# Value items' low parts behind the last counts, four pairs of one-hots instead of seven from ScalarE, one query low part later

## The reference

```python
h = relu(layernorm(x))
q, k, v = h @ Wq + bq, h @ Wk + bk, h @ Wv + bv
adj = zeros((N, N)).at[src, dst].set(1.0)
a = q @ k.T / sqrt(512)
a = a * adj + (1.0 - adj) * -1e6
x = x + softmax(a) @ v
h = relu(layernorm(x))
# deg = edges per dst, loops included; w = deg**-0.5 at both ends
h = agg(h @ W1 + b1)          # agg: segment sum over src of w * h[dst]
h = relu(gamma * (h - mean) / sqrt(var + eps) + beta)
x = x + agg(h @ W2 + b2)
```

## Time and profile before

| | |
|---|---|
| median of 3 runs | 307.28 us (307.28 to 307.28) |
| profiled execution | 307.32 us |
| its span, first to last instruction | 305.5 us |
| granted TensorE clock | 1.00 throughout |
| TensorE busy | 295.5 us, 97% |
| VectorE busy | 207.0 us, 68% |
| ScalarE busy | 159.9 us, 52% |
| GpSimd busy | 57.6 us, 19% |

### The profile page before, as it was taken

The page is one execution under the profiler, slowest core; times in us unless marked ns, Lnnn a source line. Parts: engine busy times, 40 slices in busy tenths (PEclk is TensorE's granted clock), DMA queues, the critical chain, the costliest instruction groups (busy, mean ns, idle before and its releaser), DMA issues.

```text
span 305.5 us, 4845 instructions
## 1 busy us (share of the span) xinstructions
PE 295.5 (97%) x1345; PEld 227.3 (74%) x1345; DVE 207.0 (68%) x458; ACT 159.9 (52%) x266; POOL 57.6 (19%) x103
## 2 busy tenths in 40 slices
PE   7999889899999999999999999999999999999995
PEld 6777356466665888888888888887888888878884
DVE  3899999999977557965748575568344388276311
ACT  3999967989546546445444544357523044342000
POOL 5361353000000530032131420203010044100000
PEclk9999999999999999999999999999999999999999
DMA  7806040000600309444362625313102000000321
GB/s 256 311 23 186 1 141 0 1 0 2 207 0 3 69 3 238 79 95 89 85 148 43 150 40 104 67 38 69 34 20 52 0 3 0 0 2 0 111 98 69
DMA packets 42312, 21.67 MB, mean 71 GB/s; under 512 B 35760, under 2 KB 36016, under 8 KB 42288
## 3 DMA queue, kind: packets, MB, share of 16 engines
q1 hardware_dynamic: 41744, 20.33, 26.0%
q10 hardware_dynamic: 544, 1.05, 0.9%
HBM read 10.88 MB, written 2.10 MB: 42 GB/s over the span
## 4 chain that ended last, share of the span: by engine, by line
PE 86%; DVE 7%; issue 2%; DMA 1%; DVEq 1%; ACT 1%; ACTq 0%
PE ps L989 20%; PE ps L991 19%; PE ps L990 19%; PE ps L1242 10%; PE ps L1165 8%; PE ps L1055 8%; DVE src_oh L705 2%; DMA qk_raw<-L_gnn_Wk_in 1%; PE ps L1023 1%; DVE dst_oh L707 1%; DVEq L705 1%; DVE WT L688 1%; DVE T L809 0%; DVE smx L813 0%; DVE p L821 0%
## 5 line engine op out<-in xcount | busy, mean ns | idle before, releaser
L705 DVE TENSOR_SCALAR src_oh<-iota,ecol 128x512 f16 x135 | 40.0, 349 | 3.0 <-PE ps L1055 2.5
L1055 PE MATMUL ps<-src_oh,dst_oh 128*128 x135 | 34.0, 382 | 3.7 <-DVE dst_oh L707 3.3
L1165 PE MATMUL ps<-cnt,qh 128*128 128x512 f32 x128 | 30.1, 391 | 0.3 <-ACT cnt L575 0.3
L1055 PEld LDWEIGHTS ps<-src_oh,dst_oh 128*128 x135 | 13.3, 103 | 21.9 <-issue 12.5
L1242 PE MATMUL ps<-qh,cnt 128*128 128x512 f32 x128 | 29.3, 390 | 0.0
L1165 PEld LDWEIGHTS ps<-cnt,qh 128*128 128x128 f32 x128 | 23.9, 188 | 5.6 <-DVE qh L868 0.7
L1242 PEld LDWEIGHTS ps<-qh,cnt 128*128 128x128 f32 x128 | 24.0, 188 | 5.3 <-DVE vb L970 0.3
L991 PE MATMUL ps<-v,pT 128*128 128x512 f32 x64 | 25.0, 390 | 0.0
L989 PE MATMUL ps<-v,pT 128*128 128x512 f32 x64 | 24.9, 389 | 0.0
L989 PE MATMUL ps<-hT,qh 128*128 128x512 f32 x64 | 24.9, 389 | 0.0
L990 PE MATMUL ps<-v,pT 128*128 128x512 f32 x64 | 24.9, 389 | 0.0
(11 more groups left out here) (186 smaller groups left out, 685.2 us busy)
## 6 DMA issues: line engine op xcount, KB each, us to landing
xt<-x_in SPq DMA_DIRECT2D x16, 256.0 KB, 3.3
out<-xt SPq DMA_DIRECT2D x8, 256.0 KB, 2.1
qk_raw<-L_gnn_Wk_in ACTq DMA_DIRECT2D x2, 512.0 KB, 5.0
qk_raw<-L_gnn_Wq_in SPq DMA_DIRECT2D x2, 512.0 KB, 6.8
wB_raw<-L_gnn_Wv_in SPq DMA_DIRECT2D x2, 512.0 KB, 9.0
wB_raw<-L_gnn_W_in SPq DMA_DIRECT2D x2, 512.0 KB, 4.1
w_raw<-L_gnn_W_in SPq DMA_DIRECT2D x2, 512.0 KB, 4.6
bias_row<-L_gnn_b_in SPq DMA_DIRECT2D x2, 256.0 KB, 4.7
```

What stands on the lines that cost most here:

```text
L705: dve.tensor_scalar(src_oh[:, bass.ds(slot, 1), j, :].rearrange("p a n -> p (a n)"), iota[:, :], ecol[:, bass.ds(c + j, 1)], None, ALU.is_ ...
L1055: m = pe.matmul(ps[:, i % 2, :], dst_oh[:, bass.ds(slot, 1), :, j].rearrange("p a n -> p (a n)"), lead_oh[:, i % 2, j, :] if first and ACT ...
L1165: m = pe.matmul(bank(g), qh[:, d, a, c * P:(c + 1) * P], cnt[:, d, n * HALF:(n + 1) * HALF], start=(d == 0 and a == 1), stop=last)
```

## The change

1. The low part of each of the eight value items leaves `lo_of`. ScalarE, in `hi_of`, makes a second copy of the item from PSUM, `v_raw`, in the place in SBUF where the low part is to stand, right behind the high part's copy. VectorE subtracts later, from SBUF to SBUF (`v_lo`): blocks 0 to 5 behind the low part of ("q", 1, 0), blocks 6 and 7 in turn 0 of the blocks, behind `large_flag`. TensorE's first weighted sum waits for all eight.
2. A bank that held a value item is free once `v_raw` is made; item_lo counts only the other items (`left_bank`, `nth_lo`).
3. GpSimd's additions of bv wait for six of the eight v_lo.
4. ScalarE makes the pairs of windows 3, 5, 7 and 9 alone; windows 4, 6 and 8 get their src one-hots from VectorE, and GpSimd picks the columns of four windows instead of seven.
5. VectorE makes the low part of ("q", 0, 3) (ahead[13]) behind the one-hots of window 15 instead of before them.

```diff
-ACT_LEADS = 3
-ACT_LAST = 10
+ACT_LEADS = (3, 5, 7, 9)
...
+    v, v_raw, zT, edge_i, edge_f, chunk1, hit, reach = shared(
+        [("v", [P, NT, 2, D], F32R)], [("v_raw", [P, NT, 2, D], F32)], [("zT", [P, 2, KC, N], F32R)],
...
+    def left_bank(b, end):
+        before = [other for other in items[:end] if item_bank(other) == b]
+        if not before:
+            return None
+        if before[-1][0] == "v":
+            return S["v_raw"], before[-1][1] + 1
+        return S["item_lo"], nth_lo(before[-1])
...
-        for i in range(ACT_LEADS, ACT_LAST):
+        for i in ACT_LEADS:
             lead_columns(i)
...
+        pool.wait_ge(S["v_lo"], 6)
         for t in range(XT):
             add_bv(t)
...
                 act.activation(item_dest(item, 0), item_ps(item), ACT.Copy).then_inc(S["item_hi"], 1)
+            if what == "v":
+                act.activation(v_raw[:, n, 1, :], item_ps(item), ACT.Copy).then_inc(S["v_raw"], 1)
...
-            if ACT_LEADS <= i + 1 < ACT_LAST:
+            if i + 1 in ACT_LEADS:
                 lead_onehots(i + 1)
...
             what, n, c = item
+            if what == "v":
+                return
...
+        def v_lo(blocks):
+            for n in blocks:
+                dve.wait_ge(S["item_hi"], nth(("v", n, 0)))
+                dve.wait_ge(S["v_raw"], n + 1)
+                dve.tensor_tensor(v[:, n, 1, :], v_raw[:, n, 1, :], v[:, n, 0, :].bitcast(F32),
+                                  ALU.subtract).then_inc(S["v_lo"], 1)
...
-            chunks_of(i, first, LEAD, not ACT_LEADS <= i < ACT_LAST)
+            chunks_of(i, first, LEAD, i not in ACT_LEADS)
...
         for i in range(2, NW):
-            for item in ahead[i - 2]:
+            for item in ahead[i - 2] if i < NW - 1 else []:
                 lo_of(item)
...
-        for i in range(NW - 2, NW):
+        for i in range(NW - 3, NW):
             for item in ahead[i]:
                 lo_of(item)
...
         lo_of(("q", 1, 0))
+        v_lo(range(0, 6))
...
                 large_flag()
+                v_lo(range(6, NT))
                 p16_lo(0)
...
-            if last_in(item_bank(item), i - 1):
-                pe.wait_ge(S["item_lo"], last_in(item_bank(item), i - 1))
+            left = left_bank(item_bank(item), i - 1)
+            if left:
+                pe.wait_ge(*left)
...
             pe.wait_ge(S["p_lo"], t + 1)
+            if t == 0:
+                pe.wait_ge(S["v_lo"], NT)
```

More of the change, by code:

```diff
@@ L164, in gnn_kernel @@
     Wk_in0 Wk_in1 Wq_in0 Wq_in1 wB_in0 wB_in1 w2_in0 w2_in1 w_hi w_lo
-    x_sums x_means x_squares ln_scale ln_coef h_ready item_ps item_hi item_lo uw_ready hw_second fill_ready
+    x_sums x_means x_squares ln_scale ln_coef h_ready item_ps item_hi item_lo v_raw v_lo uw_ready hw_second fill_ready
     ncol_ready lead_cols lead_dist lead_made onehots onehots_used c_done c16 loops_added adj_in0 adj_in1 adj_in2 adj_in3
@@ L187, in gnn_kernel @@
     nth = lambda item: items.index(item) + 1
+    split_items = [item for item in items if item[0] != "v"]
+    nth_lo = lambda item: split_items.index(item) + 1
     item_bank = lambda item: start.get(item, final.get(item, 2 + (items.index(item) - len(start)) % ITEM_BANKS))
-    last_in = lambda b, end: max([n for n, other in enumerate(items[:end], 1) if item_bank(other) == b] + [0])
+    def left_bank(b, end):
[5 more added lines that the diff above has]
+        return S["item_lo"], nth_lo(before[-1])
     drel = lambda i: (drel_first if i < NW // 2 else drel_second)[:, i % (NW // 2), :]
@@ L468, in lead_onehots @@
         def lead_onehots(i):
-            n = i - ACT_LEADS + 1
+            n = ACT_LEADS.index(i) + 1
             act.wait_ge(S["lead_cols"], n)
             for j in range(LEAD):
-                act.activation(lead_oh[:, i % 2, j, :], iota[:, :], ACT.Abs,
+                act.activation(lead_oh[:, n % 2, j, :], iota[:, :], ACT.Abs,
                                bias=lead_col[:, i, j:j + 1]).then_inc(S["lead_dist"], 1)
             act.wait_ge(S["lead_dist"], LEAD * n)
-            act.activation(lead_oh[:, i % 2, :, :], lead_oh[:, i % 2, :, :], ACT.Relu, bias=ones[:, 0:1],
+            act.activation(lead_oh[:, n % 2, :, :], lead_oh[:, n % 2, :, :], ACT.Relu, bias=ones[:, 0:1],
                            scale=-1.0).then_inc(S["lead_made"], LEAD)
@@ L744, in mask_level @@
                 dve.wait_ge(S["uw_ready"], 4)
-                dve.wait_ge(S["item_lo"], nth(("w", 0, 0)))
+                dve.wait_ge(S["item_lo"], nth_lo(("w", 0, 0)))
             else:
@@ L1026, in make @@
             if what == "m":
-                pe.wait_ge(S["item_lo"], nth(("t", Q, n)))
+                pe.wait_ge(S["item_lo"], nth_lo(("t", Q, n)))
             else:
-                pe.wait_ge(S["item_lo"], nth(("h", n if what == "v" else 4 * n + 3, 0)))
+                pe.wait_ge(S["item_lo"], nth_lo(("h", n if what == "v" else 4 * n + 3, 0)))
             if item == ("v", 0, 0):
@@ L1055, in chunks @@
                 m = pe.matmul(ps[:, i % 2, :], dst_oh[:, bass.ds(slot, 1), :, j].rearrange("p a n -> p (a n)"),
-                              lead_oh[:, i % 2, j, :] if first and ACT_LEADS <= i < ACT_LAST else
+                              lead_oh[:, (ACT_LEADS.index(i) + 1) % 2, j, :] if first and i in ACT_LEADS else
                               src_oh[:, bass.ds(slot, 1), j, :].rearrange("p a n -> p (a n)"), start=first and j == 0,
@@ L1065, in counts @@
                 pe.wait_ge(S["c16"], 2 * (i - 1))
-            if ACT_LEADS <= i < ACT_LAST:
-                pe.wait_ge(S["lead_made"], LEAD * (i - ACT_LEADS + 1))
+            if i in ACT_LEADS:
+                pe.wait_ge(S["lead_made"], LEAD * (ACT_LEADS.index(i) + 1))
             first, end = bounds & (NCH - 1), bounds >> 8
@@ L1107, in scores @@
                 pe.wait_ge(S["c16"], 2 * NW)
-                pe.wait_ge(S["item_lo"], nth(("q", 0, KC - 1)))
+                pe.wait_ge(S["item_lo"], nth_lo(("q", 0, KC - 1)))
             if t == 4:
-                pe.wait_ge(S["item_lo"], len(items))
+                pe.wait_ge(S["item_lo"], len(split_items))
             if t >= 2:
@@ L1173, in _ @@
                 pe.wait_ge(S["degm_ready"], 1)
-                pe.wait_ge(S["item_lo"], last_in(6, nth(("q", 1, 0))))
+                pe.wait_ge(*left_bank(6, nth(("q", 1, 0))))
                 pe.transpose(bank(6)[:, 0:P], degm[:, 0:1].to_broadcast([P, P]), ident[:, :]).then_inc(S["degm_ps"], 1)
```

2 lines of the change are left out of this document (removed).

## The result

| | before | after |
|---|---|---|
| median | 307.28 us (307.17 to 308.27, 5 runs) | 310.03 us (309.12 to 310.31, 5 runs) |
| ratio | 1 | 1.0066, 95% interval 1.0046 to 1.0085 |
| profiled execution | 307.32 us | 310.03 us |
| its span | 305.5 us | 308.1 us |

The sign was right, the size was not: +2.75 where +0.75 was forecast, outside the range of 306.9 to 309.1. (The ratio is not the quotient of the two medians, which is 1.0089.) Both kernels' times fall into two groups some 1.1 us apart, and in the traces these groups differ in start-up (before: 47 of its 82 runs in four sets are in the lower group; after: 4 of 11 in two sets); the after profile is of the upper group where the before profile is of the lower. Lower group against lower group, after is about 309.0 and before about 307.25: +1.75 is what the changed kernel takes more, start-up aside.

The account below looks back on a forecast made before the run. TensorE, busy 97% of the span, was taken as the bound, so only its holes counted. Terms +1.36 (values), -0.66 (query), +0.05 (GpSimd) and 0 gave +0.75 on 307.32: 308.07 profiled, 308.0 median; range 306.9 to 309.1.

Parts of the forecast that it names:

- mechanism of the windows: Windows 5, 7, 9: v_raw ahead of ScalarE's pair delays the pair 0.49 us, and TensorE's groups with it; taken 1.36.
- the query's low part: Window 15: moving the low part of (0,3) behind the one-hots gains 0.66 us, bounds 0.55 to 1.05.
- the low parts behind the counts: Behind the counts, VectorE's eight moved subtractions fit into two stalls and cost 0 while nothing stretches them.
- Values in windows 5, 7 and 9: The extra ScalarE copy delays these windows by 0.49, 0.45 and 0.42 us, 1.36 together, bounds 1.08 and 1.47.
- The 0.13 that I let the step between two copies absorb: Window 7: a copy's row is 0.13 us longer than its pitch; that may go, leaving 0.36 to 0.49 of delay.
- The reading of the sequencer: Window 5: after waiting for the pair, TensorE's sequencer issues one loop turn in 1.07 us; only work queued earlier hides it.
- One-hots back on VectorE: Windows 4, 6, 8: six one-hots, 1.8 us, cost nothing because VectorE is ahead after 5.4 us of subtractions removed.
- it takes 96.07 to 96.73 out of the chain: Window 15: without the low part, VectorE's last one-hots and then TensorE's last group come 0.66 us earlier.
- GpSimd: End of window 2: fewer column copies start the window targets earlier, slowing VectorE's one-hots by 0 to 0.2 us, taken 0.05.
- rival A: Behind the counts: GpSimd's additions block VectorE's last two low parts, TensorE loses 0.53 us, 308.6 in all; chance 0.25.
- Both fit: Behind the counts: six low parts (3.66 us) and two (1.22) fit VectorE's stalls of 4.06 and 1.78, by 0.40 and 0.56.
- What I held against A: A one-hot begun inside a GpSimd operation grew by only 0.09 us (0.50 against 0.41), not by the operation's rest.

Follow-up runs that it names:

- e4: The changed kernel with ScalarE's copy v_raw behind the pair of one-hots of the same turn instead of before it: 307.70 us, ratio 0.9996.
- e2: The kernel before with four pairs by ScalarE (windows 3, 5, 7, 9) instead of seven, all else as before: 307.48 us, ratio 1.0002.
- e3: The kernel before with only the low part of query item (0,3) moved behind window 15's one-hots: 307.47 us, ratio 0.9993.
- k5: e4 with window 5's pair of one-hots made by VectorE, ScalarE keeping windows 3, 7 and 9: 307.58 us, ratio 1.0001.
- e1: The change's value items' part alone, with ScalarE's seven pairs and the query item's low part as in the kernel before: 309.89 us, ratio 1.0072.
- k7: e4 without the wait of GpSimd's additions for the sixth low part, so they run beside VectorE's low parts: 313.71 us, ratio 1.0166.
- k9: e4 with GpSimd's four additions waiting for the second masking in place of the sixth low part: 308.59 us, ratio 1.0026.
- k11: The changed kernel with 8 one-column stores on VectorE behind the first mask: 309.48 us, ratio 1.0053.
- k6: The kernel before with window 5's pair made by VectorE and the query item's low part behind window 15's one-hots: 307.24 us, ratio 0.9981.
- k8: The kernel before with 16 one-column stores on VectorE behind the first mask: 308.49 us, ratio 1.0014.
- k10: k6 with 8 one-column stores on VectorE behind the first mask: 306.55 us, ratio 0.9970.

## Why the prediction was wrong, step by step

The mechanism of the windows was right. Two terms of the sum failed, the query's low part (0.22 for 0.66) and the low parts behind the counts (0.42 for 0), and two stages that the sum left out added 0.35 (the last) and 0.92 (start-up).

- **Values in windows 5, 7 and 9: right.** Forecast +0.49, +0.45, +0.42 with 1.47 as the upper bound; measured +0.49, +0.51, +0.48, 1.48. The 0.13 that I let the step between two copies absorb was not absorbed. The reading of the sequencer held: groups at 1.07, and the second group of window 7 is 0.51 late once the shift of 1.21 ahead of the window is taken out (68.63 to 70.35). e4 takes all of it away with the one copy.
- **One-hots back on VectorE: right**, 0 (e2: -0.12, all in window 3, which has none of the six).
- **The query's low part: mis-sized.** The step that failed is "it takes 96.07 to 96.73 out of the chain". It took VectorE's data path as the limit and forgot the lesson that I had drawn for TensorE from the earlier trace rows: an engine can stand idle on its sequencer, and work in front hides it. The low part had hidden 0.36 us of idle time, and the step between the one-hots went from 1.00 to 0.77. Of 0.66, 0.22 came (0.19 in e3's window 15), outside my 0.55 to 1.05. The 0.36 is no fixed price: in k5 it is 0.10, and 0.47 came. Why, is open; that it changes with instructions elsewhere is like the last stage's branch, but no run tested it here.
- **GpSimd: wrong sign, small, cause not shown.** Forecast +0.05, measured -0.17. With three copies of the lead columns fewer, the window targets begin at 42.19 where the earlier trace rows has 43.35, start-up's 0.92 included. But e1 has all seven copies, its targets begin at 43.23, and its windows 2 to 4 still gain 0.14; e2 gains 0.13 there. So the earlier targets needn't be the reason.
- **Low parts behind the counts: rival A happened.** Forecast 0; measured +0.42 at the first weighted sum, A's price was 0.53. The step that failed is "Both fit": the six did (4.06 us held them, and the masking was not late), the last two did not. The additions stretched the identity's addition by 0.58 and the two low parts by some 0.6, together more than the 0.72 that the prediction had to spare. A had expected one wait of 1.25 there; it came in two pieces. What I held against A, a one-hot that grew by only 0.09 beside GpSimd, was another case: a one-hot of 128x384 in f16 beside a GpSimd operation on 132 columns. Why that one hardly waits and a low part beside an addition of 512 fp32 columns does, no run shows. The Trainium skill, "SBUF — State Buffer", section "SBUF: two separate sides", says that a VectorE operation with two SBUF inputs (beside a GpSimd one that reads SBUF) or in a two-port mode and a GpSimd one exclude each other for a whole instruction. For the low parts the trace agrees (1.70 us per pair of operations in k7), for the one-hot of the earlier trace rows it doesn't (0.50 for 0.41), and for p_lo with its one input (1.80 for 0.69 in k9) no row shows the mode. Had I taken A as the case, the forecast would have been 308.6, still 1.4 under the result.
- **The last stage: not in the sum at all.** +0.35 from a stage whose code the change does not touch (k11 takes it out with eight stores). No row of before could have shown it, and so no term bounded it.
- **Start-up: not in the sum.** The median of before lies in the lower group, that of after in the upper, 0.92 of the 2.75. All three runs that I had were at 307.28 us, so the prediction knew of one group only. No run shows that the group depends on the change; as far as is known it is chance that the two medians of 5 runs fell in different groups.

Sum without start-up: 1.48 - 0.17 - 0.22 + 0.42 + 0.35 and -0.14 of drift between stages is +1.72 against the forecast's +0.75; the difference of 0.97 is 0.44 from the query's part, 0.42 from the low parts beside GpSimd, 0.35 from the last stage and 0.12 from the windows, less 0.22 from windows 2 to 4 and 0.14 of drift. With +1.72 the time would have been 309.04, still inside the stated range; start-up's 0.92 is what carried it out.

## What to carry to other kernels

When an operation is taken out from in front of an engine's work, ask first what its time hid, idle time of the sequencer as well as a wait; here a third of it came back. An operation put into an engine's idle time is not free if GpSimd runs beside it, and moving GpSimd's work chose here only who waits (e4, k7, k9). A place for it beside VectorE operations that nothing waits for may be better; no run tried one. A difference of 0.1% in a stage whose code is the same should be compared with a kernel that has a few dead instructions more, before it is put down to the change.

## What the runs showed of the hardware that I had not expected

- A VectorE subtraction from SBUF to SBUF and a GpSimd addition alternate instead of sharing: six subtractions 8.08 us for 3.69, four additions 6.54 for 5.05 (k7). A one-input conversion from f16 to fp32 waits too (1.80 for 0.69, k9); a maximum does not (1.22 in both).
- A branch on VectorE that skips a block costs 0.25 us of idle time or 0.60 to 0.63, and which of a row of like branches is the long one, if any, changes with the instructions before them (k6, k8, k10, k11).
- The idle time of VectorE ahead of the one-hots of window 15 is 0.36 us in nine traces and 0.10 in k5's, with the same instructions around it.
- 3.48 us without a matmul brought TensorE's granted clock from 1.00 to 0.50, and the work behind it came 1.5 us later (k7). In k8's profiled execution 2.27 us without a matmul in start-up did the same, 0.50 between 10 and 12 us, and its stages behind start-up stand 3.05 us later than before's.
- Start-up's transposes run at 0.11 or at 0.22 us each, by the execution and not by the kernel, at a granted clock that is shown as 1.00. That is the ratio of k7's matmuls at a granted 0.50 (0.43 us apart) to those at 1.00 (0.23), so a clock that the records don't tell is a possible cause; what decides it is open.
